# Row means of a layer norm's input from eight extra columns of the projection ahead of it

## The reference

```python
h = relu(x @ w1[lang] + b1[lang])            # 256 -> 64
z = x + (h @ w2[lang] + b2[lang])            # 64 -> 256
mean = z.mean(-1); var = ((z - mean) ** 2).mean(-1)
x = x + ((z - mean) * rsqrt(var + 1e-5) * gamma[lang] + beta[lang])
x = x + (x @ W[subject].T + bias[subject])   # layer 3
```

## Time and profile before

| | us |
|---|---|
| median of 3 runs | 1580.34 (1580.19 to 1582.08) |
| the profiled execution | 1579.02 |
| its span, first to last instruction | 1576.9 |
| TensorE busy in the span | 1569.8 (7916 matmuls) |
| VectorE, ScalarE, GpSimd busy | 1132.5, 931.6, 674.2 |

### The profile page before, as it was taken

One profiled execution on the slowest core, in us unless ns is written; L12 is line 12 of the kernel. 1 busy time (PEld: TensorE's weight loads), 2 busy tenths in 40 slices (PEclk: granted clock), 3 DMA queues, 4 the chain that ended last, 5 costly groups with the idle time before them and its releaser, 6 DMA issues.

```text
span 1576.9 us, 22436 instructions
## 1 busy us (share of the span) xinstructions
PE 1569.8 (100%) x7916; PEld 1339.6 (85%) x7916; DVE 1132.5 (72%) x1685; ACT 931.6 (59%) x1683; POOL 674.2 (43%) x631
## 2 busy tenths in 40 slices
PE   9999999999999999999999999999999999999999
PEld 7888888999988888888888888888888888888898
DVE  6855557788889876776777776776776776657567
ACT  5655555666666666565565666666656666555444
POOL 7865544766786441431432432342342352038000
PEclk9999999999999999999999999999999999999999
DMA  4111105455520000000010010010010010022000
GB/s 161 55 54 54 54 27 184 165 181 180 175 82 27 27 28 27 24 31 27 15 41 28 14 41 27 14 40 28 14 41 27 14 41 27 15 60 77 14 14 28
DMA packets 31012, 85.98 MB, mean 55 GB/s; under 512 B 5030, under 2 KB 10534, under 8 KB 30774
## 3 DMA queue, kind: packets, MB, share of 16 engines
q1 hardware_dynamic: 30310, 83.21, 15.3%
q0 software_dynamic: 304, 1.10, 0.2%
q10 hardware_dynamic: 288, 0.26, 0.1%
HBM read 82.46 MB, written 2.10 MB: 54 GB/s over the span
## 4 chain that ended last, share of the span: by engine, by line
PE 96%; POOL 1%; DVE 1%; DMA 0%; issue 0%; SPq 0%; ACT 0%; ACTq 0%; POOLq 0%; DVEq 0%
PE up L684 13%; PE up L683 13%; PE up L682 13%; PE sum L441 13%; PE sum L443 13%; PE sum L442 13%; PE up L441 4%; PE up L442 4%; PE up L443 4%; PE up L449 2%; PE up L451 2%; PE up L450 2%; DMA raw<-in_shared 0%; DVE gate_inputs L2029 0%; POOL shared_up L1496 0%
## 5 line engine op out<-in xcount | busy, mean ns | idle before, releaser
L1305 ACT ACTIVATE hidden_hi<-up_tile 128x512 fp32r<-128x512 f32 x256 | 161.2, 630 | 189.4 <-DVE up_tile L2147 166.8
L2152 DVE TENSOR_TENSOR hidden_lo<-up_tile,hidden_hi 128x512 fp32r<-128x512 f32 x256 | 197.8, 792 | 44.7 <-ACT hidden_hi L1305 44.7
L2142 DVE TENSOR_TENSOR gate_tile<-up,gate_tile 128x512 f32<-128x512 f32 x192 | 130.0, 687 | 138.9 <-PE up L684 138.4
L682 PE MATMUL up<-x_sums,gate_up 128*128 128x512 f32 x512 | 199.2, 389 | 0.0
L443 PE MATMUL sum<-hidden_hi,down 128*128 128x512 f32 x512 | 199.2, 389 | 0.0
L442 PE MATMUL sum<-hidden_lo,down 128*128 128x512 f32 x512 | 199.2, 389 | 0.0
L684 PE MATMUL up<-x_sums,gate_up 128*128 128x512 f32 x512 | 199.2, 389 | 0.0
L441 PE MATMUL sum<-hidden_hi,down 128*128 128x512 f32 x512 | 199.2, 389 | 0.0
L683 PE MATMUL up<-x_sums,gate_up 128*128 128x512 f32 x512 | 199.2, 389 | 0.0
L2147 DVE TENSOR_TENSOR up_tile<-up_tile,gate_tile 128x512 f32<-128x512 f32 x192 | 184.0, 985 | 2.2
L1298 ACT ACTIVATE gate_tile<-gate_tile 128x512 f32<-128x512 f32 x192 | 119.8, 632 | 90.5 <-DVE gate_tile L2142 88.2
(11 more groups left out here) (332 smaller groups left out, 4007.1 us busy)
## 6 DMA issues: line engine op xcount, KB each, us to landing
raw<-in_experts SPq DMA_DIRECT2D x64, 512.0 KB, 3.3
raw<-in_l SPq DMA_DIRECT2D x51, 512.0 KB, 3.2
raw<-in_shared SPq DMA_DIRECT2D x23, 512.0 KB, 3.3
raw<-in_w SPq DMA_DIRECT2D x8, 256.0 KB, 2.7
x<-in_xT SPq DMA_DIRECT2D x3, 512.0 KB, 9.1
l_stage<-in_l SPq DMA_DIRECT2D x3, 512.0 KB, 4.2
out<-out_stage SPq DMA_DIRECT2D x6, 256.0 KB, 2.2
gate_w<-in_gw POOLq DMA_DIRECT2D x1, 1024.0 KB, 5.1
```

The costliest lines, as they stand in the source:

```text
L682: pe.matmul(out, wh, vh, start=first, stop=False, skip_group_check=True)
L1305: A(hi[:, i], cu[:, i], ACT.Copy).then_inc(hi_done, 1)
L2142: V.tensor_tensor(t, ps, t, ALU.add).then_inc(c_done[m], 1)
L2152: V.tensor_tensor(lo[:, i], cu[:, i], hi[:, i].bitcast(f32), ALU.subtract).then_inc(lo_done, 1)
```

## The change

The weights of `l2_up_stage` get eight more columns of the value -1/256 (`w1m`, high part; 0 in the low part), so its products give minus the row mean in rows 64 to 71 of their output. VectorE copies these rows as a high part to rows 64 to 71 of a second tile `v`, and the remainder to rows 96 to 103. ScalarE writes the high part of relu(h) twice in one operation, to `u` and to `v`. The low part of w2 keeps rows 0 to 63 only; its rows 64 to 127 hold 1 in rows 64 and 96 and 0 elsewhere (`pick`), so the second down matmul adds low w2 by high h and the mean. `minus_mean`, its matmuls, the row sums and the add of x ahead go; `res_stage` adds x itself. Constants are made at steps 2, 4, 5 and 10; rows of `v` are zeroed at step 10. `b2_done` is waited for ahead of `l2_up_stage`. In unit 4 both `x_part` come ahead of the down products.

```diff
+MEAN_ROWS = 8
...
-    w1r = place("l2_w1", [P, B, 2, DT * A2], f32r, over="gate_w1")
+    pick = place("pick_rows", [P, 1], f32, over="shared_sums", skip=small + 416)
+    w1m = place("l2_w1_mean", [P, B, 2, DT, A2 + MEAN_ROWS], f32r, over="shared_sums", skip=11264)
...
-    u = place("l2_hidden_r", [2 * A2, BLK], f32r, over="raw", skip=10240)
+    uv = place("l2_hidden_r", [2 * A2, 2, BLK], f32r, over="raw", skip=10240)
+    u, v = uv[:, 0], uv[:, 1]
...
                 if i == 0:
                     pe.wait_ge(small_full, 16 * late_small)
+                    pe.wait_ge(b2_done, 1)
...
-                        last = product(unit_ps[i][0:A2, 0, c], w1r[:, b, 0, m], w1r[:, b, 1, m],
+                        last = product(unit_ps[i][0:A2 + MEAN_ROWS, 0, c], w1m[:, b, 0, dt], w1m[:, b, 1, dt],
                                        xh[:, dt, t], xl[:, dt, t], dt == 0, dt == DT - 1)
...
-            def mean_part(i, m):
-            def mean_stage(i):
-            def product_of_parts(out, t0, n):
...
             def l2_down_stage(i):
                 b0, nb, t0, c0, n = unit(i)
+                if i in (1, 2):
+                    pe.wait_ge(out_ready, 2 * i)
                 if i == END:
                     pe.wait_ge(out_ready, 6)
-                    mean_part(i, 1)
                     x_part(i, 0)
+                    x_part(i, 1)
                 pe.wait_ge(hid_relu, i + 1)
-                if i == END:
-                    mean_part(i, 0)
-                else:
-                    pe.wait_ge(x_centered, i + 1)
                 pe.wait_ge(l2_hid, i + 1)
...
-                        pe.matmul(out, w2[b][:, 0, k], u[:, c], start=i != END, stop=False, skip_group_check=True)
-                        last = pe.matmul(out, w2[b][:, 1, k], u[:, c], start=False, stop=True, skip_group_check=True)
+                        pe.matmul(out, w2[b][:, 0, k], u[:, c], start=True, stop=False)
+                        last = pe.matmul(out, w2[b][:, 1, k], v[:, c], start=False, stop=True)
                 last.then_inc(l2_down, 1)
-                if i == END:
-                    x_part(i, 1)
...
# ScalarE, late_hi, for each batch
-                A(w1r[:, b, 0], raw[:, s, 512:640], ACT.Copy)
+                A(w1m[:, b, 0, :, 0:A2], raw[:, s, 512:640].rearrange("p (t m) -> p t m", t=DT), ACT.Copy)
                 act.wait_ge(w2_centered, b + 1)
+                A(w2[b][A2:2 * A2, 1], pick[A2:2 * A2].to_broadcast([A2, D]), ACT.Copy)
                 A(w2[b][:, 0], raw[:, s, 640:896], ACT.Copy).then_inc(w_hi, 1)
# ScalarE, hid_hi_stage, for each batch of the unit
-                    last = A(u[0:A2, c], unit_ps[i][0:A2, 0, c], ACT.Relu, bias=b1[:, b:b + 1])
+                    twice = unit_ps[i][0:A2, 0, c].rearrange("p (o n) -> p o n", o=1).to_broadcast([A2, 2, S])
+                    last = A(uv[0:A2, :, c], twice, ACT.Relu, bias=b1[:, b:b + 1])
...
# GpSimd
-                lo_part(w2[b][:, 1], raw[:, s, 640:896], w2[b][:, 0]).then_inc(w_lo, 1)
-            def row_sum(i):
+                lo_part(w2[b][0:A2, 1], raw[0:A2, s, 640:896], w2[b][0:A2, 0]).then_inc(w_lo, 1)
...
# VectorE
+                if b == 0:
+                    dve.wait_ge(ident_full, 16)
+                    V.tensor_tensor(pick[:], ident[:, A2:A2 + 1], ident[:, A2 + 32:A2 + 33], ALU.add)
...
             def center_b2():
-                V.tensor_scalar(minus_mean[:], ones[:], -1.0 / D, None, ALU.mult)
                 dve.wait_ge(b2_sum, 1)
...
+            def mean_columns(h):
+                same = ones[:].rearrange("p (b t m) -> p b t m", b=B, t=DT)
+                V.tensor_scalar(w1m[:, :, h, :, A2:A2 + MEAN_ROWS], same, (-1.0 / D, 0.0)[h], None, ALU.mult)
+            def zero_rows():
+                dve.wait_ge(w_lo, PLAIN0 + L1_CH * NE1 + B)
+                linked(V.tensor_scalar(v[A2:2 * A2], ones[A2:2 * A2, 0:1].to_broadcast([A2, BLK]), 0.0, None, ALU.mult))
...
             def hid_stage(i):
-                if i != END:
-                    dve.wait_ge(mean_done, i + 1)
-                    for dt in range(DT):
-                        last = V.tensor_tensor(y[:, dt, c], x[:, dt, t0:t0 + n], unit_ps[i][:, 1, c], ALU.add)
-                    last.then_inc(x_centered, 1)
+                dve.wait_ge(l2_up, i + 1)
+                if i:
+                    dve.wait_ge(l2_down, i)
+                m, r = slice(A2, A2 + MEAN_ROWS), slice(A2 + 32, A2 + 32 + MEAN_ROWS)
+                linked(V.tensor_copy(v[m, c], unit_ps[i][m, 0, c]))
+                V.tensor_tensor(v[r, c], unit_ps[i][m, 0, c], v[m, c].bitcast(f32), ALU.subtract)
                 dve.wait_ge(hid_relu, i + 1)
...
+            hooks.setdefault(10, []).append(zero_rows)
+            for h in range(2):
+                hooks.setdefault(4 + h, []).append(lambda h=h: mean_columns(h))
```

More of the change, by code:

```diff
@@ L49 @@
 RING = [0, 1, 2, 0]
-STAGES = ["x2", "xs", "up", "mean", "within", "hid", "down", "res", "square", "scale", "var", "eps", "diag", "rstd",
+STAGES = ["x2", "up", "within", "hid", "down", "res", "square", "scale", "var", "eps", "diag", "rstd",
           "norm", "add", "x3", "x3l", "l3a", "outa", "l3b", "outb"]
 WHEN = [dict(zip(STAGES, at)) for at in (
[4 rows of a table removed]
-for u in (0, 3):
-    del WHEN[u]["xs"]
[4 rows of a table added]
 for u in (1, 2, 3):
@@ L155, in build @@
     ws = [place(f"weight_sums{s}", [P, 2, 7 * P], f32, over=f"gate_up{s}", skip=7 * K1) for s in range(PAIRS)]
-    xst = place("x_row_sum", [P, BLK], f32, over="raw", skip=14336)
-    xsr = [place(f"x_row_sum_parts{r}", [P, 2, BLK], f32r, over="weights", skip=(12 - 4 * r) * K1) for r in range(2)]
     cg = place("gate_tile", [P, 3, BLK], f32, over="weights", skip=88 * K1)
@@ L189, in build @@
     rstd = place("rstd", [P, 4], f32, over="shared_sums", skip=small + 256)
[L190 to L193, removed]
-    w1r = place("l2_w1", [P, B, 2, DT * A2], f32r, over="gate_w1")
+    b2c = place("b2_centered", [P, B, DT], f32, over="shared_sums", skip=small + 288)
+    b2s = place("b2_sum", [P, B], f32, over="shared_sums", skip=small + 352)
+    w2s = place("w2_sum", [2 * A2, 1], f32, over="shared_sums", skip=small + 384)
+    pick = place("pick_rows", [P, 1], f32, over="shared_sums", skip=small + 416)
+    w1m = place("l2_w1_mean", [P, B, 2, DT, A2 + MEAN_ROWS], f32r, over="shared_sums", skip=11264)
     y = place("y", [P, DT, BLK], f32, over="raw")
@@ L820, in l2_up_stage, with l2_down_stage @@
                 last.then_inc(l2_up, 1)
-            def mean_part(i, m):
+            def l2_down_stage(i):
                 b0, nb, t0, c0, n = unit(i)
-                out = unit_ps[i][:, m, c0:c0 + n]
-                for dt in range(DT):
-                    for part in (xh, xl):
-                        pe.matmul(out, minus_mean[:], part[:, dt, t0:t0 + n], start=dt == 0 and part is xh, stop=False,
-                                  skip_group_check=True)
-            def mean_stage(i):
[L833 to L836, removed]
@@ L837, in mean_stage @@
                 if i in (1, 2):
                     pe.wait_ge(out_ready, 2 * i)
[L839 to L845, removed]
@@ L977, in _ @@
                         pair_up(e, j, s)
-            hooks = placed({"up": l2_up_stage, "mean": mean_stage, "down": l2_down_stage, "var": var_stage,
+            hooks = placed({"up": l2_up_stage, "down": l2_down_stage, "var": var_stage,
                             "rstd": rstd_stage, "l3a": lambda i: l3_stage(i, 0), "l3b": lambda i: l3_stage(i, 1),
@@ L1476, in _ @@
             hooks = placed({"x2": lambda i: both_hi(x2_done, x2_hi, i), "x3": lambda i: both_hi(x3_done, x3_hi, i),
-                            "xs": row_sum_hi, "scale": scale_stage, "split": split_hi_part, "hid": hid_hi_stage,
+                            "scale": scale_stage, "split": split_hi_part, "hid": hid_hi_stage,
                             "square": first_square,
@@ L1828, in late_lo @@
                 lo_part(w3[b][:, 1], raw[:, s, 0:512], w3[b][:, 0])
-                lo_part(w1r[:, b, 1], raw[:, s, 512:640], w1r[:, b, 0])
-                lo_part(w2[b][:, 1], raw[:, s, 640:896], w2[b][:, 0]).then_inc(w_lo, 1)
-            def row_sum(i):
[L1834 to L1839, removed]
-                G(xst[:], x[:, 0, t0:t0 + n], x[:, 1, t0:t0 + n], ALU.add).then_inc(xs_sum, 1)
-                pool.wait_ge(xs_hi, i)
-                lo_part(xsr[i // 2][:, 1], xst[:], xsr[i // 2][:, 0]).then_inc(xs_lo, 1)
+                lo_part(w1m[:, b, 1, :, 0:A2], raw[:, s, 512:640].rearrange("p (t m) -> p t m", t=DT), w1m[:, b, 0, :, 0:A2])
+                lo_part(w2[b][0:A2, 1], raw[0:A2, s, 640:896], w2[b][0:A2, 0]).then_inc(w_lo, 1)
             def square_lo_stage(i):
@@ L2277, in hid_stage @@
                 c = slice(c0, c0 + n)
-                if i != END:
-                    dve.wait_ge(mean_done, i + 1)
-                    if i:
-                        dve.wait_ge(x3_done, DT * i)
-                    for dt in range(DT):
```

(11 more changed lines are left out.)

14 lines of the change are left out of this document (2 added, 12 removed), and 8 rows, old and new, of the table WHEN.

## The result

The changed kernel takes 1585.48 us (median of 9 runs, 1583.79 to 1585.85), the kernel before, run beside it on the same chip, 1581.65 (9 runs, 1580.19 to 1583.88). The ratio is 1.0022, 95% interval [1.0013, 1.0031]: slower by 3.8 us, where I had forecast 1.7 us faster and a range that ended at 1580.8. That range stood on a median of three runs of the kernel before, 1580.34; nine runs put it at 1581.65, so 1.3 us of the distance to the forecast of 1578.6 belong to that and not to the change.

What follows compares the result with a forecast made beforehand. TensorE, busy 1569.8 of 1576.9 us, was taken to bound the kernel. Terms -0.95 - 0.94 - 0.48 + 0.13 + 0.52 + 0.20 - 0.16 = -1.68 took 1580.34 to 1578.6 us, range 1577.0 to 1580.8.

Steps and rivals of the forecast that it cites:

- The steps ahead of unit 0: Steps 2 to 5: `pick` and two `mean_columns` on VectorE cost 0; ScalarE's pick copies charged 0.31 us once, for batch 7.
- The wait on b2_done: Ahead of unit 0's l2_up products, 12 products earlier than before: TensorE starts 0.52 us later, bounds 0.1 and 1.7.
- Unit 0's queue: VectorE and ScalarE up to unit 0's down products: l_hidden_r keeps slack 0.3 us, was 1.15; cost 0, bound 0.7.
- the width: l2_up_stage products load 72 columns, not 64: 0.003 us each, 0.13 for the 42 outside unit 4, bounds 0 and 0.25.
- Removed matmuls: Mean matmuls taken out of units 0 to 4: together 3.33 us, 2.37 ahead of unit 4, the most the change can give.
- units 1 and 2: Two mean matmuls fewer in each, 0.47 us each; the hidden parts fit under TensorE's work, so cost 0.
- rival 3: 72-column loads in l2_up_stage not hidden under the matmul ahead: 0.134 us more per product, 6.4 in all, 1585.0; chance 0.04.
- Unit 3: Mean matmuls out, -0.48 us; wider `twice` delays l_hidden_r, so a stall of 0.20 at the down products, bounds 0 and 0.5.
- Unit 4: The end: down products 0.19 us later, but the squares' sum starts 1571.50, not 1571.66; gain 0.16, bounds 0 and 0.5.
- rival 1: New waits bite harder: both x_lo caught behind GpSimd, `b2_done` costs 1.7 us, or unit 0's down products wait; 1579.2 to 1580.2; chance 0.22.
- The sign that I had named as wrong: In the trace after, ahead of unit 0's l2_up: a gap over 1 us, where some 0.5 us was expected.
- rival 4: Edit works as said, but time moves for a reason no row shows, as earlier runs did (1580.19 to 1582.08); chance 0.06.

## Why the prediction was wrong

Measured in the tail, the forecast was -1.68 us and the result +3.83. The 5.51 us between them, term by term:

**The steps ahead of unit 0, "cost 0".** This failed, by 3.73 us (178.95 less 175.22). The step is the paragraph on steps 2 to 5, with the charge of 0.31 us for the copies of batch 7 alone: between them they left VectorE's steps 2 to 8 at no other cost, and the long centrings are in its steps 4 and 6. I had read in the earlier trace rows that VectorE and GpSimd take turns, and costed the edit's new VectorE operations by it. I put no term in the sum for what the edit does to GpSimd's own: a low part on 64 partitions takes the same 0.74 us as one on 128, and by that length it looks free. I took as given that a waiting VectorE operation gets in behind the GpSimd operation at hand. In the eight kernels here with the low part on all rows it does: of 81 waits of 0.15 us or more of `hidden_lo`, the centrings and x_lo (their length less their shortest, from step 0 to 55 us behind it) none sat through an end of a GpSimd operation. In the six with 64 partitions VectorE sat through seven such ends per trace, in five of them, and through five in the sixth. By the Trainium skill, "SBUF — State Buffer", section "SBUF: two separate sides", VectorE, with two inputs from SBUF, and GpSimd share a pair of ports, which goes for a whole instruction to the one that starts first while the other blocks; every wait here does end with the end of a GpSimd instruction, so the traces agree, but with 64 partitions it may be the second or third end and not the first.

**The wait on b2_done, 0.52.** Within its bounds: alone in the kernel before it costs 1.0 us; taken out of the run with the low part on all rows (with the columns moved to step 1) it gives 0.48 back, and waits for the next term come in its place. I had b2_centered end 0.68 us earlier, as `minus_mean` was moved away, at 0.18 us length. Measured from step 0 it ends at 51.41 us with the low part on all rows, at 51.31 in the kernel before: it starts earlier but takes 0.49 us, since now it, and no longer `minus_mean`, waits out GpSimd's last part. The gain of the moved operation went to the GpSimd operation that it had been waiting for.

**Unit 0's queue, "slack 0.3, cost 0".** This failed too. With -0.95, +0.04 for the width and +0.52, unit 0 was to bring 0.39 us. With the low part on all rows it costs 0.74: steps 9 to 20 grow by 0.31 us and hold unit 1's gain of 0.43. The step that failed is that I followed l_hidden_r to unit 0's down-products and stopped. VectorE's copies and zeros also push its following tile, the residual and the squares, and these the variance's products wait for. Both terms together are 1.13 us of the gap, and since taking the wait out returned 0.48, about what I had charged for it, it is the queue that was mis-sized.

**Removed matmuls, width, units 1 and 2.** Right. Units 1 and 2 each gain 0.43 to 0.44 us; 0.47 less 12 times 0.003 is 0.43. The 72-column products start 0.117 us apart in units 1 and 2 and 0.123 in unit 3, where the 64-column ones took 0.114 and 0.120; rival 3 falls.

**Unit 3, -0.26 in all.** Wrong in sign: +0.21. The stall for l_hidden_r is there as forecast: the first down-product starts 0.30 us after the matmul ahead of it and not 0.12, so 0.18 in place of 0.20 (too short an idle time for the list of waits; the 0.3 us for l_hidden_r in that list are unit 4's). But TensorE, early after the gains, also waits 0.4 us for x_lo ahead of unit 3's up-products, which I had not looked at. **Unit 4, -0.16**: measured +0.03, at the edge of its bounds (0 to 0.5 of gain); the down-products start 0.2 later as forecast (ScalarE's doubled copy takes 0.66 and the single one 0.46), but the sum of the squares starts 0.04 earlier, counted from step 39, where I had 0.16.

Together 3.73 + 1.13 + 0.47 + 0.19 = 5.52. The new waits, rival 1, were the right place with too low a ceiling: it had VectorE held at the two x_lo alone, not at centrings steps ahead and through two more operations. The sign that I had named as wrong, a gap over 1 us ahead of unit 0's up-products, is what came.

What stays open: why an operation on 64 partitions changes at which end VectorE gets in. It isn't only the operation at hand: the centring above began in a 128-partition operation and sat through its end. I tried no other counts of partitions, nor rows 64 to 127 in place of 0 to 63.

## What to carry to other kernels

Where VectorE and GpSimd contend, an edit that changes how many partitions a GpSimd operation covers can change VectorE's queue, even if its own duration stays the same (making one strided changed nothing here): look for VectorE operations much longer than their shortest. Before crediting matmuls taken out, follow every engine's queue past the first consumer until the next wait of TensorE: here three of five units, 0, 3 and 4, lost their gain to VectorE's or ScalarE's queue. Put a wait where its value is used and not earlier; one line cost 1.0 us, and another, in every unit where only the first needed it, 5.5.

## What the runs showed of the hardware

**A GpSimd operation on 64 partitions takes what one on 128 takes** (0.74 us), and VectorE's on 8 partitions what one on 128 takes (0.69 us for 512 columns).

**The clock falls also where TensorE never stands still, and not in every execution.** The windows from 308 us, before and after:

```profile
308.00:336.00 28.00, 28.00 (x236) 28.00 (x236) 22.27 (x48) 16.41 (x37) 14.26 (x17) 1.00 0.45 161
```

```profile
308.00:336.00 28.00, 28.00 (x211) 28.00 (x211) 19.69 (x43) 14.44 (x33) 12.42 (x15) 0.88 0.41 142
```

TensorE is busy throughout, and in both traces it has no wait of over 0.3 us from 240 us to step 0. Over the fourteen profiled executions this window has one of three clocks, and step 0 starts accordingly: 1.00 and 1401.8 to 1402.2 us, 0.94 and 1402.7 to 1404.0, 0.88 and 1404.7 to 1405.0. The kernel before, profiled at 1.00, is one of the fastest; the run with one wait added to it too. These are the 3.2 us ahead of step 0, and most of the scatter of either kernel's runs: of the runs of the kernel before that stood beside the experiments, the 14 with a mean clock of 1.000 took 1579.0 to 1580.1 us and the 45 with 0.998 1581.1 to 1584.1. Why the clock falls there in some executions stays open. I had called it a reason that no row shows (rival 4); a row of the windows shows it.
